# Experts' rows scattered to token order by GpSimd, read by attention without positions or gathers

## The reference

```python
xn = layernorm(x)
# attention, causal, over 2048 tokens of each of the 8 sequences
q, k, v = split(xn @ W_qkv)                  # 256 -> 3 x 256
attn = softmax(mask(q @ k.T / 16)) @ v
# shared expert
shared = (silu(xn @ sg) * (xn @ su)) @ sd     # 256 -> 512 -> 256
# one routed expert of 32 for each token
logits = xn @ gate_w; e = argmax(logits); xs = xn * sigmoid(max(logits))
routed = (silu(xs @ rg[e]) * (xs @ ru[e])) @ rd[e]
out = x + attn + shared + routed
```

## Time and profile before

| what | us |
|---|---|
| median of 3 runs (2383.94 to 2389.36) | 2385.42 |
| the profiled execution's own time | 2384.18 |
| its span, from the first instruction to the last | 2382.2 |
| TensorE busy in the span | 2316.4 (97%) |
| VectorE, ScalarE, GpSimd busy | 1565.0, 1216.2, 1065.6 |

### The profile page before, as it was taken

How to read it: one execution, slowest core, us unless ns; L and a number is a source line. 1 busy time by engine, 2 the same in 40 slices (tenths; PEclk the granted TensorE clock), 3 DMA queues, 4 the chain that set the end, 5 groups by cost and what they waited for, 6 DMA issues and landing times. The chain is left out here.

```text
span 2382.2 us, 48635 instructions
## 1 busy us (share of the span) xinstructions
PE 2316.4 (97%) x16118; PEld 2136.5 (90%) x16118; DVE 1565.0 (66%) x3322; ACT 1216.2 (51%) x2254; POOL 1065.6 (45%) x1031
## 2 busy tenths in 40 slices
PE   7999999999978999999999997999999999999998
PEld 6888888888868999999999995898988888888888
DVE  6777777777757777777777774646455555555555
ACT  3344434444425556656655653555555555555545
POOL 2333332333323333333333330666666666666667
PEclk9999999999998999999999999999999999999999
DMA  6665566665556766776767776334343444434331
GB/s 221 217 213 200 205 219 226 213 209 204 203 190 218 239 231 235 243 235 229 243 233 230 243 239 233 103 100 134 117 138 119 132 127 128 139 120 161 123 114 51
DMA packets 301977, 439.23 MB, mean 184 GB/s; under 512 B 35968, under 2 KB 209792, under 8 KB 301824
## 3 DMA queue, kind: packets, MB, share of 16 engines
q1 hardware_dynamic: 283712, 398.90, 48.9%
q0 software_dynamic: 18112, 38.37, 6.0%
HBM read 288.21 MB, written 148.96 MB: 184 GB/s over the span
## 5 line engine op out<-in xcount | busy, mean ns | idle before, releaser
L1231 POOL TENSOR_TENSOR t_p_lo<-t_score,t_p_hi 128x512 fp32r<-128x512 f32 (+1 forms) x320 | 360.0, 1131 | 190.7 <-ACT t_score L1355 113.9
L884 POOL DMA_INDIRECT ahead_rows<-xs_rows,ahead_slot x160 | 182.7, 1142 | 417.8 <-DMA ahead_slot<-token_of 257.7
L1347 ACT COPY t_score<-t_psS 128x512 f32<-128x512 f32 (+1 forms) x320 | 167.5, 523 | 332.5 <-PE t_psS L71 229.7
L1428 PE MATMUL t_psO<-t_v_hi,t_p_hi 128*128 128x258 f32 x1088 | 318.3, 293 | 0.9 <-DVE t_outb L1309 0.9
L1430 PE MATMUL t_psO<-t_v_hi,t_p_lo 128*128 128x258 f32 x1088 | 307.6, 283 | 0.0
L1432 PE MATMUL t_psO<-t_v_lo,t_p_hi 128*128 128x256 f32 x1088 | 306.6, 282 | 0.0
L1285 DVE TENSOR_TENSOR t_top<-t_top,t_psS 128x512 f32<-128x512 f32 (+3 forms) x264 | 155.1, 587 | 167.6 <-ACT t_score L1347 163.0
L305 POOL DMA_INDIRECT token_of<-a_token_i,a_slot_i x128 | 141.6, 1107 | 242.9 <-DVE a_slot_i L415 213.7
L69 PE MATMUL t_psS<-t_q_hi,ahead_x_hi 128*128 128x512 f32 (+3 forms) x640 | 233.8, 365 | 6.5 <-DVE t_q_lo L1267 5.5
L71 PE MATMUL t_psS<-t_q_lo,ahead_x_hi 128*128 128x512 f32 (+3 forms) x640 | 233.6, 365 | 0.0
L70 PE MATMUL t_psS<-t_q_hi,ahead_x_lo 128*128 128x512 f32 (+3 forms) x640 | 232.9, 364 | 0.0
(11 more groups left out here) (187 smaller groups left out, 7334.9 us busy)
## 6 DMA issues: line engine op xcount, KB each, us to landing
ahead_raw<-in_L_ffn_routed_gate_w SPq DMA_DIRECT2D x42, 512.0 KB
ahead_raw<-in_L_ffn_routed_up_w SPq DMA_DIRECT2D x42, 512.0 KB
ahead_raw<-in_L_ffn_routed_down_w SPq DMA_DIRECT2D x41, 512.0 KB, 5.0
e_raw<-in_L_ffn_routed_gate_w SPq DMA_DIRECT2D x41, 512.0 KB
e_raw<-in_L_ffn_routed_up_w SPq DMA_DIRECT2D x41, 512.0 KB
e_raw<-in_L_ffn_routed_down_w SPq DMA_DIRECT2D x41, 512.0 KB, 4.8
routed_rows<-e_dout SPq DMA_DIRECT2D x80, 256.0 KB, 4.4
a_xt<-in_L_attn_x SPq DMA_DIRECT2D x32, 512.0 KB, 5.9
```

Of the source, the lines that this page charges most:

```text
L884: g.indirect_dma_start(out=xg[:, k, h], out_offset=None, in_=xs, in_offset=bass.IndirectOffsetOnAxis(slot[:, k, h:h + 1], 0)).then_inc(x_i ...
L1231: g_.tensor_tensor(p_lo[:, t % LR, c0:], score[:, t % SR, c0:], p_hi[:, t % HR, c0:].bitcast(F32), ALU.subtract).then_inc(lo_ok, 1)
L1347: s.copy(score[:, t % SR, c0:], psS[:, n % BANKS, c0:]).then_inc(u_act, 1)
L1428: nc.tensor.matmul(psO[:, a, 0:W], p_hi[:, kp, cols], v_hi[:, kv, j % J], start=j == 0, stop=False, skip_group_check=True)
```

## The change

- The table `token_of` now begins as numbers 16384 to 16639 (an iota in place of a memset), 256 different ones for each tile, and has 256 places more. An unused place so names one of 256 spare rows, which `xs_rows` and `routed_rows` now have behind the 16384 real ones. The spare rows of `xs_rows` are stored as zero once (`nobody`). The 32 stores of zero to `routed_rows` are gone.
- `one_hot` and `rank` keep only two groups and one; `shift` is gone.
- In the expert stage the store of a tile is replaced: SP loads the tile's places again (`load_back`, into `slot_back`), and GpSimd writes the 256 rows to their own tokens' places by two indirect DMAs (`scatter`), behind the gather of its step.
- In the attention stage `positions`, `position_sum` and `gather` are gone. SP loads the routed rows beside the shared ones; it first waits for `rows_ok`, which GpSimd raises when all scatters have landed.

```diff
@@ token_stage, SP
-            sp.wait_ge(zeroed, 4)
+            sp.wait_ge(zeroed, 5)
             for n in range(n_zero):
...
+            sp.dma_start(token_of[E * NT * P:E * NT * P + ST].rearrange("(p c) o -> p (c o)", p=1),
+                         nothing[0:1, 0:ST]).then_inc(zero_out, 16)
+            sp.dma_start(xs[NT * P:NT * P + ST].rearrange("(p h) d -> p (h d)", p=P), nobody[:]).then_inc(zero_out, 16)
...
-                if NT * P // ST + i < ET:
-                    sp.dma_start(d_t[NT * P // ST + i], nothing[:, 0:ST * D // P].bitcast(F32)
-                                 .rearrange("p (h d) -> p h d", h=ST // P)).then_inc(rest_out, 16)
...
-            sp.wait_ge(rest_out, 16 * (ET - NT * P // ST))
@@ token_stage, GpSimd
             rstd_of(0)
-            p_.memset(nothing[:], 0).then_inc(zeroed, 1)
+            p_.iota(nothing[:], pattern=[[0, 1024 // ST], [1, ST]], base=NT * P, channel_multiplier=0).then_inc(zeroed, 1)
+            p_.memset(nobody[:], 0.0).then_inc(zeroed, 1)
@@ token_stage, VectorE, tile_tables
-                then(v.tensor_tensor(shift[:], tiles_cum[:], tiles[:], ALU.subtract))
-                then(v.tensor_scalar(shift[:], shift[:], float(ST), None, ALU.mult))
@@ expert_stage, SP
-            def store(t, k):
-                wait(sp, do_ok, t + 1)
-                sp.dma_start(d_t[t], dout[:, k]).then_inc(d_out[k], 16)
+            def load_back(t, k, i):
+                if not is_first(i):
+                    wait_apart(sp, d_out[k], 16 * H * i, passed)
+                first = sp.value_load(keep.tile_slots[0:1, bass.ds(t, 1)], min_val=0, max_val=NS - 1)
+                sp.dma_start(slot_back[:, k], token_t[first]).then_inc(back_in[k], 16)
...
                 load_slots(t + 2, k, i + 1)
                 load_up(t + 3, 1 - k)
+                load_back(t, k, i)
                 load_down(t + 2, k)
-                if not is_first(t):
-                    store(t - 1, 1 - k)
             R = tiles(sp, step)
-            load_transposed(0)
-            store(R * 2 + 1, 1)
-            for g in range(1, ahead.x_hi.shape[1]):
+            for g in range(ahead.x_hi.shape[1]):
                 load_transposed(g)
...
-                wait_apart(sp, d_out[k], (R + 1) * 16, passed)
@@ expert_stage, GpSimd
+            def scatter(t, k, i):
+                wait(pool, do_ok, t + 1)
+                wait_apart(pool, back_in[k], 16 * (i + 1), passed)
+                for h in range(H):
+                    g.indirect_dma_start(out=d_rows, out_offset=bass.IndirectOffsetOnAxis(slot_back[:, k, h:h + 1], 0),
+                                         in_=dout[:, k, h], in_offset=None).then_inc(d_out[k], 16)
             def step(t, k, i):
                 high_down(t, k, i)
                 gather(t + 2, k, i + 1)
+                if not is_first(t):
+                    scatter(t - 1, 1 - k, i - 1 + k)
             R = tiles(pool, step)
+            scatter(R * 2 + 1, 1, R)
@@ attention_stage, SP
                 sp.dma_start(xr[:, k], sh_g[g][:, 2 * h:2 * h + 2]).then_inc(r_in[k], 16)
+                sp.dma_start(routed[:, k], d_g[g][:, 2 * h:2 * h + 2]).then_inc(r_in[k], 16)
...
-            for g in range(2):
-                load_rows(g)
             for g in range(VR):
                 load_v(g)
+            sp.wait_ge(rows_ok, 1)
+            for n in range(2):
+                load_rows(n)
@@ attention_stage, GpSimd
-            pool.wait_ge(pos_ok, 1)
-            gather(0)
-            gather(1)
+            last = pool.value_load(keep.last_pair[0:1, 0:1], min_val=1, max_val=ET // 2 - 1)
+            for k in range(2):
+                wait_apart(pool, ahead.d_out[k], (last + 1) * (16 * ST // P), passed)
+            pool.sem_inc(rows_ok, 1)
@@ attention_stage, VectorE
-                if 2 <= step < 2 * NP + 2:
-                    positions(step - 2)
-                elif step == 2 * NP + 2:
-                    position_sum()
```

More of the change, by code:

```diff
@@ L128, in token_stage @@
         expert_f = sb("expert_f", [P, E])
-        one_hot, rank, shift = keep.one_hot, keep.rank, keep.shift
+        one_hot = sb("one_hot", [P, 2, J, E], BF16)
+        rank = sb("rank", [P, J])
+        nobody = sb("nobody", [P, ST * D // P])
         seen = sb("seen", [P, 2, J, E])
@@ L764, in _, with expert_stage @@
                     down(i, 3)
-def expert_stage(nc, xs, rgw, ruw, rdw, d_t, token_t, xth_g, xtl_g, keep, ahead, D, F, E, ET):
+def expert_stage(nc, xs, rgw, ruw, rdw, d_rows, token_t, xth_g, xtl_g, keep, ahead, D, F, E, ET):
     C, H, IT = D // P, ST // P, F // P
@@ L798, in expert_stage @@
         w_in, wd_in, x_in, slot_in = ahead.w_in, ahead.wd_in, ahead.rows_in, ahead.slot_in
-        d_out = [sem(f"d_out{k}") for k in range(2)]
+        d_out = ahead.d_out
+        back_in = [sem(f"back_in{k}") for k in range(2)]
         passed = sem("passed")
@@ L964, in d_copy @@
                 wait(act, d_mm, t + 1)
-                wait(act, d_out[k], 16 * i)
+                wait(act, d_out[k], 16 * H * i)
                 s.copy(dout[:, k], psD[:]).then_inc(do_ok, 1)
@@ L1100, in last_keys, with attention_stage @@
         return self.s_unit[self.last_pv(g)]
[L1103 removed]
+def attention_stage(nc, sh_g, d_g, xth_g, xtl_g, vh_g, vl_g, out_g, keep, ahead, D, B, N, ET):
     C, NB, GB = D // P, N // P, N // GT
@@ L1132, in attention_stage @@
         negmax = sb("negmax", [P, J])
-        E = keep.one_hot.shape[2]
-        NP = B * NB * E // GT
-        moved = score[:, SR - 2]
-        start = score[:, SR - 1, 0:B * NB]
         spread = sb("spread", [P, J, P], F32R)
@@ L1150, in attention_stage @@
         r_in = [sem(f"r_in{k}") for k in range(2)]
-        d_in = [sem(f"d_in{k}") for k in range(2)]
+        rows_ok = sem("rows_ok")
         o_out = [sem(f"o_out{k}") for k in range(2)]
@@ L1209, in _ @@
             g_ = nc.gpsimd
-            def gather(r):
-                k = r % 2
-                wait(pool, base_ok, r - 1)
-                wait_apart(pool, d_in[k], 16 * (r // 2), passed)
-                g_.indirect_dma_start(out=routed[:, k], out_offset=None, in_=d_rows,
-                                      in_offset=bass.IndirectOffsetOnAxis(keep.position[:, r:r + 1], 0)).then_inc(d_in[k], 16)
             def add_up(r):
-                k, n = r % 2, r // 2
-                wait(pool, r_in[n % 2], 16 * (n // 2 + 1))
-                wait(pool, d_in[k], 16 * (r // 2 + 1))
+                n = r // 2
+                wait(pool, r_in[n % 2], 32 * (n // 2 + 1))
                 wait(pool, o_ok, r - BR + 1)
-                g_.tensor_tensor(base[:, r % BR], routed[:, k], xr[:, n % 2, r % 2], ALU.add).then_inc(base_ok, 1)
-                if r + 2 < R:
-                    gather(r + 2)
+                g_.tensor_tensor(base[:, r % BR], routed[:, n % 2, r % 2], xr[:, n % 2, r % 2], ALU.add).then_inc(base_ok, 1)
             def p_low(t):
@@ L1249, in _ @@
             v = nc.vector
-            def positions(m):
-                ts = slice(m // 2 * GT // E, (m // 2 + 1) * GT // E)
-                wait(dve, pos_step, m)
-                if m % 2 == 0:
-                    v.tensor_tensor(moved.rearrange("p (t e) -> p t e", e=E), keep.one_hot[:, ts],
-                                    keep.shift[:].unsqueeze(1).to_broadcast([P, GT // E, E]), ALU.mult).then_inc(pos_step, 1)
-                else:
-                    v.tensor_reduce(start[:, ts], moved.rearrange("p (t e) -> p t e", e=E), AX.X, ALU.add).then_inc(pos_step, 1)
-            def position_sum():
-                dve.wait_ge(pos_step, 2 * NP)
-                v.tensor_tensor(keep.position[:], start, keep.rank[:], ALU.add).then_inc(pos_ok, 1)
             def q_low(g, c):
@@ L1470, in __init__ @@
         self.rows_in = [sem(f"rows_in{k}") for k in range(2)]
+        self.d_out = [sem(f"d_out{k}") for k in range(2)]
 class Keep:
```

50 lines of the change are left out of this document (22 added, 28 removed).

## The result

The changed kernel takes 2410.24 us (median of 4 runs, 2408.55 to 2411.45), the kernel before 2384.68 (4 runs): ratio 1.0102 [1.0089, 1.0115], slower by 25 us. I had said 2403, with 2377 to 2409 as the range: the sign was right, and the time lies 1.2 us outside. The profiled execution took 2409.29 us with a span of 2407.2.

The account below looks back on a forecast made before the run. TensorE was taken to bound the kernel, other engines counting only through its gaps. 2384.18 + 25 - 2.3 - 5.3 + 1.1 - 0.3 = 2402.4, median 1.2 above, so 2403.6, said as 2403; range 2377 to 2409 us.

Parts of the forecast that it names:

- Expert stage, +25: Expert steps: scatters delay GpSimd's cast, which holds VectorE's second weight remainder; TensorE stalls 0.32 us over 78 steps, 25 us.
- The forecast step: One expert step: second scatter ends at 1011.98, cast runs to 1013.03, second remainder ends at 1014.12 for 1012.96.
- s settles at 0.64 - s: Expert steps: first is 0.64 us late; a stall s gives VectorE's chain that head start, so s becomes 0.32 us.
- The third rival: Expert step: first scatter asked for after 1009.91, both scatters held up; 12 us, 2391 us, slower; chance 0.12.
- The first rival: Expert step: VectorE keeps its turn, the cast waits through remainder and h_low; stage costs 0, 2378.6 us; chance 0.2.
- a lock held from the DMA over to the cast: Expert step: VectorE issued first yet was blocked, read as GpSimd's port lock lasting from indirect DMA through cast.
- Boundary, -2.3: Between experts and attention: SP's loads end sooner, last scatters' landing is not waited for; 2.3 us gained, bounds 0 to 3.5.
- Attention, -5.3: Attention's end: without gathers, p_low is over before the next spread, so TensorE's waits go; gain 5.3 us, bounds 0 to 6.5.
- The three spread waits: Attention's end: three places where TensorE waits for VectorE's spread, slowed beside GpSimd's p_low and add; 5.3 us.
- Token stage, +0.8: Token stage: iota and larger memset delay the first normalisation, +1.1 us; the two shift instructions go, -0.3 us.
- the forecast's own range: Whole kernel: 2396 to 2411 us, from a stall of 0.25 to 0.4 us a step and the small terms' bounds.
- the chances for slower: Whole kernel: slower by over 0.2% given 0.66 over the listed cases, brought to 0.6 for the unseen.

Follow-up runs that it names:

- alone: The kernel before with only attention's part of the change (routed rows read in direct transfers, no positions or gathers): 2378.94 us, ratio 0.9981.
- no last scatters: The kernel of x early without the four indirect writes of the last two tiles, whose rows 64 direct stores zero in the token stage: 2373.19 us, one run.
- last rows later: Changed kernel with the cast ahead of the scatters, and the very last tile's two scatters moved into attention's program: 2371.77 us, ratio 0.9949.
- x early: Changed kernel with the cast ahead of the scatters, and attention's five transposed-x loads moved to SP's first four expert steps: 2388.00 us, ratio 1.0016.

## Why the prediction came out as it did

**Expert stage, +25: right in mechanism, short by 4.3 us.** The forecast step had the cast 0.24 us behind the second remainder and the remainder at 2.38 us; it was 0.36 and 2.50. The stall was 29.3 / 78 = 0.38 us a step for 0.32, inside the 0.25 to 0.4 given. It is a mean over unlike steps, 0.6 us and 0.1 us in turn. "s settles at 0.64 - s" was a slip: a rule by which each stall is 0.64 less the one before doesn't settle but swings about 0.32, as the steps do, and has the same mean. The view shows TensorE waiting for `x_low` in 32 steps of 78, not in most. Two details were wrong and offset each other. The first scatter starts 0.84 us after the copy's end, not 0.4. And so the second one meets no remainder that matters (0.98 us, not 1.48). That both fell out of the sum was luck. The third rival needed the first scatter to come behind the first remainder's start; it came ahead of it in 75 of 76 steps, by up to 0.19 us.

**The first rival, VectorE keeps its turn, was wrong in its price.** In two runs VectorE did keep it in every step seen, by the wait for h, and they cost 17.3 and 29.5 us, not 0. The rival had the cast wait through `h_low` as well and hurt only the down remainder, inside its slack; in the runs the cast ran behind the remainder and held `h_low` 0.85 us, which is too much. These two runs also say that a held remainder isn't the only way in which a late cast costs: with the remainder free, the stage was 29.5 us longer all the same. The Trainium skill (SBUF — State Buffer, Who interferes with whom) has "Issue order, not op shape, decides who blocks." With the wait, the trace agrees: the remainder 0.27 to 0.34 us ahead stays at 1.22 us. Behind a scatter it agrees only if issue means the time at which a cast with its waits met queued up on GpSimd: the recorded starts say the opposite order (1203.22 and 1203.58). So my reading of the earlier trace rows, a lock held from the DMA over to the cast, was wrong: the run in which the cast waits behind the scatters rules it out.

**Boundary, -2.3: the step that failed, by 8.6 us.** SP did what was forecast: its loads ended 2.3 us after TensorE's last matmul had ended, where it was 5.9. The step that failed is GpSimd's end, put at its last descriptors ("1445.4 to 1447.6, their landing is not waited for here"). That was read from the program, and as far as the program's waits go it holds. But the block's end waits for GpSimd's DRAIN, and that ended 9.3 us behind the last descriptors. The forecast had no term for it, and the bounds, 0 to 3.5, had no case on the slow side. The kernel before held the evidence: at the end of its token stage GpSimd's last gather ended at 708.89, SP was through at 712.1, and TensorE's first transpose came at 714.98, right behind GpSimd's DRAIN:

```profile
L95 POOLq DRAIN  x1: 9408/9408/9408, 705.3 to 705.3; - x1
```

At the end of the expert stage the kernel before hides its DRAIN, since GpSimd's last instruction there ends at 1436.2, 8 us before TensorE's. The change took both away: GpSimd's last work now waits for ScalarE's copy behind the last matmul, and the DRAIN behind it is more than twice as long.

**Attention, -5.3: right.** It was -6.3 in the changed kernel and -6.1 alone. The three spread waits gave 4.9 of it.

**Token stage, +0.8: wrong by 5 us.** The start came as forecast in kind: the iota took 0.98 us, the fill 0.52, the first normalisation 1.98 us for 1.46 (forecast 2.5), and TensorE's first transpose 0.54 us late. The forecast had no term for the 9.3 KB per partition that left the table kept over all stages, which moved every later tensor: -4.4 us in the loop.

By terms: 18.2 forecast, 4.3 + 8.6 - 5.1 - 1.0 = 6.8 missed, 25.0 measured. That the time lies only 1.2 us outside the range is luck: the token loop's gain, which nobody forecast, hides half of the boundary's miss. The upper bound was also drawn low: the forecast's own range went to 2411, which would have held the 2410.24, the one of 8 in 10 only to 2409. And the chances for slower add up to 0.68, not 0.66; nothing hangs on that.

## What to carry to other kernels

Put an indirect DMA behind GpSimd's casts, not ahead of one that VectorE's order depends on: the same 160 scatters cost 29 us at one place and nothing at the other. Let GpSimd come to the end of its block early when it has issued indirect DMAs in it, so that its DRAIN lies beside other engines' work; here, carry the last rows over into the next block. When a forecast says that an engine gets there earlier, ask as well which other engine the end of the block waits for, and what it did last.

## What the runs showed of the hardware

- GpSimd's DRAIN at the end of a block takes long when the block has issued indirect DMAs, and it does so whether the last of them was just made or not. What I read of it (us; each line one execution, its number of indirect DMAs counted in the trace):

```
                           indirect DMAs   DRAIN   began                         ended behind the last descriptors
attention stage, after     0               0.6     -                             -
attention stage, before    128             1.9     35 behind the last            36.9
expert stage, before       160             4.0     3.3 behind the last           7.3
token stage, before        132             9.4     before the last's end         5.8
experts, no last scatters  316             8.2     3.4 behind the last           11.6
experts, last rows later   318             9.2     before the last's end         8.4
experts, x early           320             10.3    before the last's end         8.6
expert stage, after        320             11.0    before the last's end         9.3
```

  In the expert stage the part of it that lies behind the last descriptors is about twice as long with twice as many indirect DMAs (4.0 us in all four executions with 160, 8.2 to 9.5 in those with 316 to 320). That is a correlation: no run varied their number alone, and the 128 gathers of the attention stage left 1.9. The rows had landed well before the DRAIN ended: the last packet of their queue moved 1.1 us behind the last descriptors with x early, and 4.7 us behind them in the changed kernel, where loads of x stood beside them. What the DRAIN waits for stays open.
- Where GpSimd's DRAIN was over early, in the kernel before, the next block's first matmul came 1.2 us after SP's last issue.
- A VectorE instruction with both inputs in SBUF that starts up to 0.4 us before the recorded start of a GpSimd cast is held until 1.09 us after its end, if the cast stood queued behind an indirect DMA with its waits met; where the cast still waited for a semaphore, VectorE went first, 153 times of 153.
- Moving the same tensors by up to 9.3 KB within a partition changed a loop of 32 groups from 651.6 to 647.2 us, 0.7%, with nearly the same instructions, and moving them back gave 651.2. Which pair of tensors does it stays open.
